# Striking scores in PSUM with TensorE, and moving their reading and two additions to other engines

## The chip, the cores and the metric

The kernel runs on one core of a Trainium2 chip. The metric is the device time of one execution in microseconds; several executions are timed and their median is compared. One more execution was profiled; all rows below come from it.

## The reference

The input is 8 sequences of 512 tokens with 128 features. After a layer norm, `xn` goes into two branches whose results meet in `x + s * silu(f)`.

- `s`: an attention block with three sources (blocks of 4 tokens, 64 selected tokens, windows of 32), gated, projected and normalised.
- `f`: a product-key expert layer. This is the part that the change touches:

```python
q = (x @ Wq.T).reshape(b, n, 2, HEADS, DIM_KEY).transpose(2, 0, 1, 3, 4)
sim = jnp.einsum('pbnhd,hkpd->pbnhk', q, keys)        # 2 x 8 heads x 32 scores for a token
sx, ix = jax.lax.top_k(sim[0], TOPK)                  # the 16 largest of 32
sy, iy = jax.lax.top_k(sim[1], TOPK)
all_scores = (sx[..., :, None] + sy[..., None, :]).reshape(b, n, HEADS, TOPK * TOPK)
scores, pk_indices = jax.lax.top_k(all_scores, TOPK)
wd = W_down[pk_indices]
wu = W_up[pk_indices]
h = jax.nn.gelu(jnp.einsum('bnd,bnhkd->bnhk', x, wd), approximate=False)
h = h * jax.nn.softmax(scores, axis=-1)
return jnp.einsum('bnhk,bnhkd->bnd', h, wu)
```

`pk_indices` is a place in the 16 x 16 table of rank pairs, and only 50 pairs can be among the 16 largest sums, so 50 experts are enough.

## The kernel before

A tile is 128 tokens; there are 32, four to a sequence (a batch row). Each of the five engines runs a program of its own, written out by hand, and they meet at counting semaphores. From tile 4 on all of them run `turn(n)`, whose four forms j = 0 to 3 belong to the four tiles of a row; a turn also works on tiles n-1 to n-4, so a tile passes through a pipeline of five turns. Attention steps of the row are spread over the same turns.

The steps of tile n, in order:

1. TensorE, `scores`: 16 vectors of 32 scores for a token into PSUM bank `sim_bank[n % 2]`, 128 x 512. It waits for `sim_used` of tile n-2.
2. VectorE, `first_8`: 16 MAX8 instructions, the 8 largest of each vector, into `top[:, v, 0:8]`. `mark_above`: 1 in the bf16 tile `above` where a score is at least the eighth.
3. VectorE, `strike_above`: `rest` = score - 1e38 x mark, in SBUF.
4. VectorE, `sum_above`, `spill_above`, `put_ties`: the marks are counted, and 8 extra columns of `rest` get the eighth value as often as ties ask for it. The counts and the products of the counting lie in columns of the score's own PSUM bank, which is free by then; `put_ties` gives it back (`sim_used`).
5. VectorE, `next_8`: 16 MAX8 over the 40 columns of `rest`, ranks 9 to 16.
6. TensorE transposes the ranks (`top_columns`), ScalarE copies them out, TensorE forms the 50 gaps of each head (`pair_gaps`), ScalarE copies them into `gap[n % 4]`; VectorE finds the 16th smallest (`gaps_of_pairs`, `gaps_of_thirds`, `last_gaps`).
7. GpSimd, `past_of`: gap minus that, f32, into `past`. ScalarE, `side_of`: its sign, bf16, into `side`. TensorE transposes that (`transpose_sides`), ScalarE copies it to `sideT` (`take_sides`), GpSimd squares it (`square_of`), TensorE counts with both (`count_places`), ScalarE (`out_by_of`) and GpSimd (`drop_of`) drop the pairs that are out.
8. ScalarE takes the exponentials with their sums (`exps`, eight for a tile), VectorE inverts the sums (`invert_sums`), GpSimd weighs (`weigh`), adds head halves (`add_halves`, 8 heads to 4) and quarters (`add_quarters`, 4 to 2); TensorE transposes the two that are left (`expert_weights`). For the last four tiles TensorE adds some or all of the heads in PSUM instead.

VectorE's turn n is `strike_above(n)`, half of `first_8(n + 1)`, `sum_above`, `invert_sums(n - 4)`, `spill_above`, in j = 0 the row maxima of the attention scores, the other half of `first_8`, `put_ties`, `mark_above(n + 1)`, half of `next_8`, the gaps of tile n-1 with the other half between them.

The last tile takes `last_past_of` on VectorE instead of `past_of`, and ScalarE squares its sides from PSUM.

Of the kernel before, what the change touches and what calls it, by code (L numbers as in the profile page):

```python
# [83 lines left out]
def program(nc, x, wq, bq, wk, bk, wv, bv, wo, bo, wg, bg, wc, bc, ws, bs,  # L84
# [16 lines left out]
    with ctx:  # L101
# [6 lines left out]
        def sem(name):  # L108
# [112 lines left out]
        rest = sb("rest", [P, VECS, KEYS + 8])  # L221
# [4 lines left out]
        past = sb("past", [P, HEADS, CANDS])  # L226
        side = sb("side", [P, HEADS, CANDS], BF16)
# [8 lines left out]
        wgt4 = sb("wgt4", [P, HEADS // 2, CANDS])  # L236
        wgt2 = [sb(f"wgt2_{i}", [P, 2, CANDS]) for i in range(2)]
# [37 lines left out]
        above_done, struck, summed_above, spill_done = (  # L275
            sem(n) for n in ("above_done", "struck", "summed_above", "spill_done"))
        topT_ready, topT_out, gap_ready, gap_out = (sem(n) for n in ("topT_ready", "topT_out", "gap_ready", "gap_out"))
        slot_gap_done, last8_done, past_done, side_done = (
            sem(n) for n in ("slot_gap_done", "last8_done", "past_done", "side_done"))
# [7 lines left out]
        wgt_done, wgt4_done, wgt2_done, c_ready, c_out = (  # L287
            sem(n) for n in ("wgt_done", "wgt4_done", "wgt2_done", "c_ready", "c_out"))
# [106 lines left out]
        def _(pool):  # L395
# [13 lines left out]
            nc.gpsimd.tensor_copy(ident16[:, :], ident[:, :])  # L409
            nc.gpsimd.tensor_scalar(off_mean[:, :], ident[:, :], -1.0 / D, None, ALU.add)  # L410
# [108 lines left out]
            def add_halves(n):  # L519

                pool.wait_ge(wgt_done, n + 1)
                w = wgt[n % 2]
                nc.gpsimd.tensor_tensor(wgt4[:, :, :], w[:, 0:HEADS // 2, :], w[:, HEADS // 2:HEADS, :],  # L523
                                        ALU.add).then_inc(wgt4_done, 1)

            def add_quarters(n):
                pool.wait_ge(wgt4_done, n + 1)
                if n >= 2:
                    pool.wait_ge(c_ready, n - 1)
                nc.gpsimd.tensor_tensor(wgt2[n % 2][:, :, :], wgt4[:, 0:2, :], wgt4[:, 2:4, :],  # L530
                                        ALU.add).then_inc(wgt2_done, 1)
# [77 lines left out]
            def turn(n):  # L609
                b, j = divmod(n, TB)  # L610
                if j == 0:
# [4 lines left out]
                    add_quarters(n - 4)  # L616
# [4 lines left out]
                elif j == 1:  # L621
# [4 lines left out]
                    add_quarters(n - 4)  # L626
                    square_of(n - 2)
                elif j == 2:
# [6 lines left out]
                    add_quarters(n - 4)  # L635
                    square_of(n - 2)
                    norm2(b - 1)
                elif n < TILES - 1:
# [7 lines left out]
                    add_quarters(n - 4)  # L646
                    if b >= 2:
                        add_input(b - 2)
                else:
# [3 lines left out]
                    add_quarters(n - 4)  # L653
# [53 lines left out]
        def _(act):  # L707
# [23 lines left out]
            def side_of(n):  # L731

                if n < TILES - 1:
                    act.wait_ge(past_done, n + 1)
                else:
                    act.wait_ge(last_past, 1)
                if n >= 1:
                    act.wait_ge(sideT_ready, n)
                nc.scalar.activation(side[:, :, :], past[:, :, :], ACT.Sign).then_inc(side_done, 1)  # L739

# [8 lines left out]
            def take_sides(n):  # L749

                act.wait_ge(sideT_ready, n + 1)
                if n == TILES - 1:
                    nc.scalar.activation(last_sideT[0:TWO, :], t_bank[0:TWO, :], ACT.Copy).then_inc(sideT_out, 1)
# [66 lines left out]
            side_of(0)  # L820
# [96 lines left out]
            def last_squares():  # L917
                nc.scalar.activation(last_squareT[0:TWO, :], t_bank[0:TWO, :], ACT.Square).then_inc(last_square, 1)
# [67 lines left out]
            def turn(n):  # L986
                b, j = divmod(n, TB)
                if j == 0:
# [3 lines left out]
                    side_of(n - 2)  # L992
# [9 lines left out]
                elif j == 1:  # L1002
# [3 lines left out]
                    side_of(n - 2)  # L1006
# [8 lines left out]
                elif j == 2:  # L1015
                    out_by_of(n - 3)
                    side_of(n - 2)
# [10 lines left out]
                elif n < TILES - 1:  # L1028
# [3 lines left out]
                    side_of(n - 2)  # L1032
# [6 lines left out]
                else:  # L1039
# [3 lines left out]
                    side_of(n - 2)  # L1043
# [11 lines left out]
            side_of(1)  # L1055
# [15 lines left out]
            side_of(TILES - 2)  # L1071
# [5 lines left out]
            side_of(TILES - 1)  # L1077
# [17 lines left out]
        def _(dve):  # L1095
# [76 lines left out]
            def mark_above(n):  # L1172

                dve.wait_ge(sim_top8, n + 1)
                if n >= 1:
                    dve.wait_ge(summed_above, n)
                nc.vector.tensor_tensor(above[:, :, :], sim_bank[n % 2][:, :].rearrange("p (v k) -> p v k", k=KEYS),  # L1177
                                        eighth(n, KEYS), ALU.is_ge).then_inc(above_done, 1)

            def strike_above(n):  # L1180

                dve.wait_ge(above_done, n + 1)
                if n >= 1:
                    dve.wait_ge(top_done, 2 * n)
                nc.vector.scalar_tensor_tensor(rest[:, :, 0:KEYS], above[:, :, :], STRUCK,  # L1185
                                               sim_bank[n % 2][:, :].rearrange("p (v k) -> p v k", k=KEYS),
                                               ALU.mult, ALU.add).then_inc(struck, 1)

            def sum_above(n):

                dve.wait_ge(struck, n + 1)
# [3 lines left out]
            def tie_slots(n):  # L1195
                return sim_bank[n % 2][:, TIES:TIES + 8 * VECS].rearrange("p (v k) -> p v k", v=VECS)
# [9 lines left out]
            def put_ties(n):  # L1206

                dve.wait_ge(spill_done, n + 1)
                nc.vector.scalar_tensor_tensor(rest[:, :, KEYS:KEYS + 8], tie_slots(n), SPILL, eighth(n, 8),
                                               ALU.mult, ALU.min).then_inc(sim_used, 1)  # L1210

            def next_8(n, h):
                dve.wait_ge(sim_used, n + 1)
                for v in range(h * HALF_V, (h + 1) * HALF_V):
                    last = nc.vector.max(top[n % 3][:, v, 8:16], rest[:, v, :])  # L1215
# [135 lines left out]
            def turn(n):  # L1351
                b, j = divmod(n, TB)
                strike_above(n)
                if n + 1 in tiles:
                    first_8(n + 1, [0])
                sum_above(n)
                invert_sums(n - 4)
                spill_above(n)
                if j == 0:
                    maxima(b - 1)  # L1360
                if n + 1 in tiles:
                    first_8(n + 1, [1])
                put_ties(n)
                if n + 1 in tiles:
# [25 lines left out]
            def last_past_of(m):  # L1390
                dve.wait_ge(last8_done, m + 1)
                dve.wait_ge(side_done, m)
                nc.vector.tensor_tensor(past[:, :, :], gap[m % 4][:, :, :],
# [116 lines left out]
        def _(pe):  # L1510
# [61 lines left out]

            def top_columns(n):
# [18 lines left out]
            def transpose_sides(n):  # L1592
                pe.wait_ge(side_done, n + 1)
# [5 lines left out]
                for k in range(HEADS // 2):  # L1599
                    last = mm(dst[0:TWO, bass.ts(k, P)], side[:, 2 * k:2 * k + 2, :].rearrange("p h c -> p (h c)"),  # L1600
# [17 lines left out]
            def expert_weights(n):  # L1618
# [9 lines left out]
                if n < TILES - TB:  # L1628
                    pe.wait_ge(wgt2_done, n + 1)
                    last = nc.tensor.transpose(o, wgt2[n % 2][:, :, :].rearrange("p h c -> p (h c)"), ident[:, :])  # L1630
                else:
                    if n == TILES - TB:
                        pe.wait_ge(wgt4_done, n + 1)
                        w, heads = wgt4, HEADS // 2
                    elif n < TILES - 1:
                        pe.wait_ge(wgt_done, n + 1)
                        w, heads = (wgt if n < TILES - LAST else last_wgts)[n % 2], HEADS
                    else:
# [352 lines left out]
```

## Time and profile before

| | |
|---|---|
| median of 3 runs | 278.73 us (277.35 to 278.85) |
| the profiled execution | 277.19 us, its span 275.4 us |
| VectorE (DVE) busy | 261.0 us, 95% |
| TensorE (PE) busy | 237.8 us, 86% |
| ScalarE (ACT) busy | 234.9 us, 85% |
| GpSimd (POOL) busy | 225.9 us, 82% |
| mean granted TensorE clock | 0.988 of full speed |

The span goes from the first to the last instruction; the execution's own time is 1.8 us longer. Busy time of an engine is the time in which an instruction of its own runs, waits left out. The first 58 us are set-up and the first four tiles; then come seven rows of four turns; the last 27 us finish what is left in the pipeline.

### The profile page before, as it was taken

To read this page: it belongs to the slowest core of one execution; us is meant where nothing else is said; L and a number is where in the kernel's file an instruction comes from. 1 tells how busy PE (TensorE), PEld (TensorE's weight loads), DVE (VectorE), ACT (ScalarE), POOL (GpSimd) and SP (SyncE) were. 2 spreads that over 40 slices of the span, in tenths; PEclk is the share of its full clock that TensorE was granted. 3 is DMA by queue.
4 is the path that set the end of the run, shared out by engine and by line. 5 is a ranking of instruction groups with operands and counts; after the bars stand their busy time and mean duration, and the time that the engine had idled before them with its cause. 6 is when DMAs were issued, how large, how long until landed. Compare 5 with 4: busy or idle time off the path is not lost.

```text
span 275.4 us, 7038 instructions
## 1 busy us (share of the span) xinstructions
PE 237.8 (86%) x1562; PEld 176.2 (64%) x1562; DVE 261.0 (95%) x1715; ACT 234.9 (85%) x1048; POOL 225.9 (82%) x344
## 2 busy tenths in 40 slices
PE   7799689897989988988898889988998899898891
PEld 7456343685668666765676577657765776587780
DVE  5899999999999999999999999999999999998985
ACT  2553866989899999999989999999999999998953
POOL 7889701467588979998999889988998899889972
PEclk9999999999899999999999999999999999999997
DMA  7930000000000000100000000100010001000102
GB/s 179 281 80 1 2 0 0 2 1 0 5 0 0 5 0 1 38 6 0 2 12 31 1 0 2 42 0 5 0 39 4 1 0 40 2 1 4 38 4 76
DMA packets 11228, 6.23 MB, mean 23 GB/s; under 512 B 1457, under 2 KB 10674, under 8 KB 11186
## 3 DMA queue, kind: packets, MB, share of 16 engines
q1 hardware_dynamic: 9858, 5.12, 7.0%
q10 hardware_dynamic: 1328, 0.66, 1.1%
q8 instruction: 13, 0.21, 0.3%
q14 instruction: 29, 0.24, 0.3%
HBM read 3.67 MB, written 2.10 MB: 21 GB/s over the span
## 4 chain that ended last, share of the span: by engine, by line
POOL 29%; PE 29%; ACT 22%; issue 14%; DVE 5%; POOLq 0%; ACTq 0%; DVEq 0%
POOL past L487 4%; PE scratch L1662 4%; PE sim L1570 4%; POOL squareT L502 4%; ACT prob L847 3%; POOL drop L509 3%; POOL wgt L515 3%; PE s_bank L1764 3%; PE s_bank L1758 2%; ACT gap L769 2%; ACT spare L866 2%; PE t_bank L1588 2%; PE s_bank L1553 2%; POOL wgt L523 2%; ACT side L739 2%
## 5 line engine op out<-in xcount | busy, mean ns | idle before, releaser
L1215 DVE MAX8 top<-rest 128x8 f32<-128x40 f32 x512 | 57.4, 191 | 0.1
L1165 DVE MAX8 top<-sim 128x8 f32<-128x32 f32 x496 | 54.0, 184 | 0.0
L847 ACT ACTIVATE prob<-drop 128x50 f32<-128x50 f32 x224 | 51.5, 254 | 0.0
L847 ACT ACTIVATION_READ_ACCUMULATOR prob<-drop 128x1 f32 x224 | 46.9, 211 | 0.0
L502 POOL TENSOR_TENSOR squareT<-sideT 100x512 bf16<-100x512 bf16 x31 | 32.6, 1050 | 4.8 <-ACT sideT L757 4.8
L487 POOL TENSOR_TENSOR past<-gap,last 128x400 f32<-128x400 f32 x31 | 26.8, 864 | 9.5 <-DVE last L1239 9.5
L1570 PE MATMUL sim<-sim_w,xT_all 128*128 128x512 f32 x64 | 33.9, 611 | 0.5 <-ACT xT_all L794 0.5
L509 POOL TENSOR_TENSOR drop<-gap,out_by 128x400 f32<-128x400 f32 x30 | 31.0, 1033 | 1.2 <-ACT out_by L746 1.2
L1588 PE MATMUL t_bank<-gaps_of,topT 128*128 128x200 f32 x128 | 30.1, 359 | 2.0 <-ACT topT L762 2.0
L515 POOL TENSOR_TENSOR wgt<-prob,rden 128x400 f32<-128x400 f32 x30 | 25.7, 856 | 5.9 <-DVE rden L1157 5.9
L1239 DVE MAX8 last<-slot_gap 128x8 f32<-128x22 f32 x256 | 24.4, 169 | 1.1
L1588 PEld LDWEIGHTS t_bank<-gaps_of,topT 128*128 128x128 f32 x128 | 20.8, 193 | 5.5 <-ACT topT L762 3.2
L1192 DVE TENSOR_REDUCE sim<-above 128x16 f32<-128x512 bf16 x32 | 21.9, 683 | 0.1
L1177 DVE TENSOR_TENSOR above<-sim,top 128x512 bf16<-128x512 f32 x32 | 21.8, 683 | 0.1
L1614 PE MATMUL f_bank<-count_s,sideT 101*128 101x100 bf16 x124 | 15.1, 208 | 7.8 <-POOL squareT L502 7.8
L1185 DVE SCALAR_TENSOR_TENSOR rest<-above,sim 128x512 f32<-128x512 bf16 x32 | 21.4, 669 | 0.1
L1614 PEld LDWEIGHTS f_bank<-count_s,sideT 101*128 101x128 bf16 x124 | 11.5, 98 | 15.1 <-issue 14.9
L757 ACT ACTIVATE sideT<-f_bank 100x512 bf16<-100x512 f32 x31 | 18.8, 607 | 0.7 <-PE f_bank L1600 0.5
L769 ACT ACTIVATE gap<-t_bank 128x400 f32<-128x400 f32 x32 | 16.1, 503 | 3.5 <-PE t_bank L1588 2.1
L739 ACT ACTIVATE side<-past 128x400 bf16<-128x400 f32 x32 | 17.1, 536 | 1.9 <-POOL past L487 1.8
L523 POOL TENSOR_TENSOR wgt<-wgt 128x200 f32<-128x200 f32 x29 | 17.7, 609 | 1.2
L1600 PE MATMUL f_bank<-ident,side 128*100 128x128 bf16 x124 | 13.1, 229 | 5.6 <-ACT side L739 5.3
(295 smaller groups left out, 755.7 us busy)
## 6 DMA issues: line engine op xcount, KB each, us to landing
out<-y_sb SPq DMA_DIRECT2D x7, 256.0 KB, 2.3
x_sb<-in_L_attn_hidden_states SPq DMA_DIRECT2D x2, 256.0 KB, 3.8
fwq_sb<-in_L_ffn_Wq ACTq DMA_DIRECT2D x2, 256.0 KB, 5.6
x_sb<-in_L_attn_hidden_states SPq DMA_DIRECT2D x1, 512.0 KB, 5.3
wc_sb<-in_L_attn_Wc SPq DMA_DIRECT2D x1, 256.0 KB
out<-last_y SPq DMA_DIRECT2D x2, 128.0 KB, 1.9
wo_in<-in_L_attn_Wo SPq DMA_DIRECT2D x1, 192.0 KB
keys_sb<-in_L_ffn_keys ACTq DMA_DIRECT2D x1, 128.0 KB, 3.3
```

What stands on the lines that cost most here:

```text
L487: nc.gpsimd.tensor_tensor(past[:, :, :], gap[n % 4][:, :, :], last8[n % 2][:, :, 7:8].to_broadcast([P, HEADS, CANDS]), ALU.subtract).then_ ...
L502: nc.gpsimd.tensor_tensor(squareT[0:TWO, :], sideT[0:TWO, :], sideT[0:TWO, :], ALU.mult).then_inc(square_done, 1)
L509: nc.gpsimd.tensor_tensor(drop[:, :, :], gap[n % 4][:, :, :], out_by[:, :, :], ALU.add).then_inc(drop_done, 1)
L515: nc.gpsimd.tensor_tensor(w[:, :, :], prob[n % 2][:, :, :], rden[n % 2][:, :].unsqueeze(2).to_broadcast([P, HEADS, CANDS]), ALU.mult).then ...
L523: nc.gpsimd.tensor_tensor(wgt4[:, :, :], w[:, 0:HEADS // 2, :], w[:, HEADS // 2:HEADS, :], ALU.add).then_inc(wgt4_done, 1)
L847: last = nc.scalar.activation(prob[d][:, h, :], drop[:, h, :], ACT.Exp, scale=-1.0, accum_out=den[d][:, h:h + 1])
L1165: last = nc.vector.max(top[n % 3][:, v, 0:8], sim_bank[n % 2][:, bass.ts(v, KEYS)])
L1215: last = nc.vector.max(top[n % 3][:, v, 8:16], rest[:, v, :])
L1239: last = nc.vector.max(last8[n % 2][:, h, :], slot_gap[:, h, :])
L1570: mm(sim_bank[n % 2][:, :], xT_all[:, bass.ts(n, P)], sim_w[:, :], start=True, stop=True).then_inc(sim_ready, 1)
L1588: last = mm(t_bank[:, bass.ts(k, HALF_H * CANDS)], topT[:, bass.ts(k, P)], gaps_of[:, :, :].rearrange("p h c -> p (h c)"), start=True, sto ...
L1614: mm(o, one[0:TWO + 1, bass.ts(k, P)], count_s[0:TWO + 1, :], start=True, stop=False)
```

## The change

- TensorE's new `strike(n)` adds -1e38 x mark to the scores where they lie in PSUM, with a constant `strike16` that GpSimd makes at the start. ScalarE's new `take_struck(n)` copies the struck scores to `rest[n % 2]`, now two buffers, and gives the bank back. Both stand first in their engine's turn. In tiles 0 to 3 VectorE still strikes.
- The counts (`counts`) and what `spill_above` makes (`tie`) now lie in SBUF. On VectorE `strike_above` leaves the turn, `spill_above` comes ahead of `invert_sums`, and `put_ties` ahead of the second half of `first_8`.
- `side_of` is gone: `past` is bf16, TensorE transposes it as it is, and ScalarE takes the sign when it copies the transposed differences out of PSUM.
- `add_quarters` is gone: TensorE adds the two pairs of heads in PSUM with two accumulating matmuls against the identity, where it transposed one pair.
- The last tile's differences are taken from the gaps in PSUM, and the square of its signs from `last_sideT`.

```diff
+        rest = [sb(f"rest{i}", [P, VECS, KEYS + 8]) for i in range(2)]
+        strike16 = sb("strike16", [P, P], BF16)
+        counts = sb("counts", [P, VECS])
+        tie = sb("tie", [P, VECS, 8])
-        side = sb("side", [P, HEADS, CANDS], BF16)
+        past = sb("past", [P, HEADS, CANDS], BF16)
+            nc.gpsimd.tensor_scalar(strike16[:, :], ident[:, :], STRUCK, None, ALU.mult)
...
             def past_of(n):
-                    pool.wait_ge(side_done, n)
+                    pool.wait_ge(sideT_ready, n)
...
-            def side_of(n):
-                nc.scalar.activation(side[:, :, :], past[:, :, :], ACT.Sign).then_inc(side_done, 1)
...
-                nc.scalar.activation(sideT[0:TWO, :], f_bank[0:TWO, :], ACT.Copy).then_inc(sideT_out, 1)
+                nc.scalar.activation(sideT[0:TWO, :], f_bank[0:TWO, :], ACT.Sign).then_inc(sideT_out, 1)
+
+            def take_struck(n):
+                act.wait_ge(struck, n - TB + 1)
+                act.wait_ge(top_done, 2 * n - 2)
+                nc.scalar.activation(rest[n % 2][:, :, 0:KEYS], sim_bank[n % 2][:, :].rearrange("p (v k) -> p v k", k=KEYS),
+                                     ACT.Copy).then_inc(sim_used, 1)
...
             def mark_above(n):
+                    if n <= TB:
+                        dve.wait_ge(sim_used, n)
+                    else:
+                        dve.wait_ge(struck, n - TB)
...
             def sum_above(n):
-                nc.vector.tensor_reduce(sim_bank[n % 2][:, 0:TIES], above[:, :, :], AX_X, ALU.add
-                                        ).then_inc(summed_above, 1)
+                nc.vector.tensor_reduce(counts[:, :], above[:, :, :], AX_X, ALU.add).then_inc(summed_above, 1)
...
-                nc.vector.scalar_tensor_tensor(tie_slots(n),
-                                               sim_bank[n % 2][:, 0:TIES].unsqueeze(2).to_broadcast([P, VECS, 8]), 2.0,
+                nc.vector.scalar_tensor_tensor(tie[:, :, :], counts[:, :].unsqueeze(2).to_broadcast([P, VECS, 8]), 2.0,
                                                rank_row[:, 7:15].unsqueeze(1).to_broadcast([P, VECS, 8]),
...
-                nc.vector.scalar_tensor_tensor(rest[:, :, KEYS:KEYS + 8], tie_slots(n), SPILL, eighth(n, 8),
-                                               ALU.mult, ALU.min).then_inc(sim_used, 1)
+                nc.vector.scalar_tensor_tensor(rest[n % 2][:, :, KEYS:KEYS + 8], tie[:, :, :], SPILL, eighth(n, 8),
+                                               ALU.mult, ALU.min).then_inc(ties_done, 1)
...
             def turn(n):
-                strike_above(n)
+                sum_above(n)
                 if n + 1 in tiles:
                     first_8(n + 1, [0])
-                sum_above(n)
+                spill_above(n)
                 invert_sums(n - 4)
-                spill_above(n)
                 if j == 0:
                     maxima(b - 1)
+                put_ties(n)
                 if n + 1 in tiles:
                     first_8(n + 1, [1])
-                put_ties(n)
...
+            def strike(n):
+                pe.wait_ge(above_done, n + 1)
+                mm(sim_bank[n % 2][:, :], strike16[:, :], above[:, :, :].rearrange("p v k -> p (v k)"),
+                   start=False, stop=True, skip_group_check=True).then_inc(struck, 1)
...
             def expert_weights(n):
-                    last = nc.tensor.transpose(o, wgt2[n % 2][:, :, :].rearrange("p h c -> p (h c)"), ident[:, :])
+                    pe.wait_ge(wgt4_done, n + 1)
+                    w, heads = wgt4[n % 2], HEADS // 2
+                for h in range(0, heads, 2):
+                    last = mm(o, w[:, h:h + 2, :].rearrange("p h c -> p (h c)"),
+                              ident[:, :], start=(h == 0), stop=(h == heads - 2))
```

## Rows read from the trace of the kernel before

**Rows 1.** Windows of one batch row: busy us (instructions), then clock, DMA share.
```profile
162.95:191.10 28.15, 24.91 (x171) 19.01 (x171) 27.53 (x196) 27.12 (x132) 26.28 (x36) 1.00 0.04 12
```
**Rows 2.** Timeline, VectorE: start us, us, line, operation; one row, first and last turn.
```profile
57.91 0.63 DVE L1185 SCALAR_TENSOR_TENSOR rest<-above,sim 128x512 f32<-128x512 bf16 x1
...
163.63 0.68 DVE L1185 SCALAR_TENSOR_TENSOR rest<-above,sim 128x512 f32<-128x512 bf16 x1
...
164.22 0.89 DVE L1165 MAX8 top<-sim 128x8 f32<-128x32 f32 x8
...
165.73 0.30 DVE L1201 SCALAR_TENSOR_TENSOR sim<-sim,rank_row 128x128 f32<-128x128 f32 x1
...
166.72 0.28 DVE L1209 SCALAR_TENSOR_TENSOR rest<-sim,top 128x128 f32<-128x128 f32 x1
...
166.91 0.69 DVE L1177 TENSOR_TENSOR above<-sim,top 128x512 bf16<-128x512 f32 x1
...
170.28 0.67 DVE L1185 SCALAR_TENSOR_TENSOR rest<-above,sim 128x512 f32<-128x512 bf16 x1
...
178.35 0.67 DVE L1185 SCALAR_TENSOR_TENSOR rest<-above,sim 128x512 f32<-128x512 bf16 x1
...
185.00 0.67 DVE L1185 SCALAR_TENSOR_TENSOR rest<-above,sim 128x512 f32<-128x512 bf16 x1
...
248.08 0.68 DVE L1185 SCALAR_TENSOR_TENSOR rest<-above,sim 128x512 f32<-128x512 bf16 x1
```
**Rows 3.** Timeline, ScalarE, third turn of the row.
```profile
187.33 0.55 ACT L739 ACTIVATE side<-past 128x400 bf16<-128x400 f32 x1
...
189.66 0.62 ACT L757 ACTIVATE sideT<-f_bank 100x512 bf16<-100x512 f32 x1
```
**Rows 4.** Timeline, TensorE, first turn of the row, and the tail.
```profile
171.13 0.30 PE L1696 MATMUL s_bank<-win_mask,ident 128*128 128x320 bf16 x1
...
171.26 1.01 PE L1700 MATMUL s_bank<-kw,qw 128*128 128x80 f32 x8
...
262.61 0.68 PE L1642 MATMUL sim<-ident,wgt 128*100 128x128 f32 x4
```
**Rows 5.** Timeline, GpSimd, the same row.
```profile
165.29 1.28 POOL L600 TENSOR_TENSOR y<-y,s_norm 128x512 f32<-128x512 f32 x1
...
171.49 0.88 POOL L487 TENSOR_TENSOR past<-gap,last 128x400 f32<-128x400 f32 x1
...
174.93 0.39 POOL L530 TENSOR_TENSOR wgt<-wgt 128x100 f32<-128x100 f32 x1
...
175.28 1.04 POOL L502 TENSOR_TENSOR squareT<-sideT 100x512 bf16<-100x512 bf16 x1
...
180.04 1.03 POOL L509 TENSOR_TENSOR drop<-gap,out_by 128x400 f32<-128x400 f32 x1
...
185.98 0.86 POOL L487 TENSOR_TENSOR past<-gap,last 128x400 f32<-128x400 f32 x1
```
**Rows 6.** Timeline, VectorE, tail.
```profile
257.28 1.62 DVE L1393 TENSOR_TENSOR past<-gap,last 128x400 f32<-128x400 f32 x1
...
269.05 1.22 DVE L1423 SCALAR_TENSOR_TENSOR nmr<-mv,rstd 128x2 f32<-128x2 f32 x1 [0.33 <-POOL rstd L698]
...
270.19 0.41 DVE L1468 SCALAR_TENSOR_TENSOR half_f<-f_bank,s_norm 128x256 f32<-128x256 f32 x1
...
270.63 0.42 DVE L1475 SCALAR_TENSOR_TENSOR last_y<-tanh_f,half_f 128x256 f32<-128x256 f32 x1
```
**Rows 7.** Timeline, GpSimd, tail.
```profile
257.20 1.27 POOL L606 TENSOR_TENSOR y_sb<-y,x_sb 128x512 f32<-128x512 f32 x1
...
258.43 1.37 POOL L502 TENSOR_TENSOR squareT<-sideT 100x512 bf16<-100x512 bf16 x1
...
268.98 1.26 POOL L606 TENSOR_TENSOR y_sb<-y,x_sb 128x512 f32<-128x512 f32 x1
```
**Rows 8.** Timeline, GpSimd, start.
```profile
2.71 0.55 POOL L410 TENSOR_SCALAR off_mean<-ident 128x128 f32<-128x128 f32 x1
```

More of the change, by code:

```diff
@@ L235, in program @@
         wgt = [sb(f"wgt{i}", [P, HEADS, CANDS]) for i in range(2)]
-        wgt4 = sb("wgt4", [P, HEADS // 2, CANDS])
-        wgt2 = [sb(f"wgt2_{i}", [P, 2, CANDS]) for i in range(2)]
+        wgt4 = [sb(f"wgt4_{i}", [P, HEADS // 2, CANDS]) for i in range(2)]
         last_drop = [sb(f"last_drop{i}", [P, HEADS, CANDS]) for i in range(2)]
@@ L286, in program @@
         half_out = sem("half_out")
-        wgt_done, wgt4_done, wgt2_done, c_ready, c_out = (
-            sem(n) for n in ("wgt_done", "wgt4_done", "wgt2_done", "c_ready", "c_out"))
+        wgt_done, wgt4_done, c_ready, c_out = (
+            sem(n) for n in ("wgt_done", "wgt4_done", "c_ready", "c_out"))
         last_past, last_square, last_kept, last_wgt, blocks_scaled = (
@@ L521, in add_halves @@
                 pool.wait_ge(wgt_done, n + 1)
[L522 to L527, printed above, removed]
                 if n >= 2:
                     pool.wait_ge(c_ready, n - 1)
-                nc.gpsimd.tensor_tensor(wgt2[n % 2][:, :, :], wgt4[:, 0:2, :], wgt4[:, 2:4, :],
-                                        ALU.add).then_inc(wgt2_done, 1)
+                w = wgt[n % 2]
+                nc.gpsimd.tensor_tensor(wgt4[n % 2][:, :, :], w[:, 0:HEADS // 2, :], w[:, HEADS // 2:HEADS, :],
+                                        ALU.add).then_inc(wgt4_done, 1)
             def gelu_times_weights(b):
@@ L752, in take_sides @@
                 if n == TILES - 1:
-                    nc.scalar.activation(last_sideT[0:TWO, :], t_bank[0:TWO, :], ACT.Copy).then_inc(sideT_out, 1)
+                    nc.scalar.activation(last_sideT[0:TWO, :], t_bank[0:TWO, :], ACT.Sign).then_inc(sideT_out, 1)
                     return
@@ L1627, in expert_weights @@
                 o = dst[0:TWO, bass.ts(n % TB, P)]
-                if n < TILES - TB:
-                    pe.wait_ge(wgt2_done, n + 1)
-                    last = nc.tensor.transpose(o, wgt2[n % 2][:, :, :].rearrange("p h c -> p (h c)"), ident[:, :])
-                else:
[L1632 to L1638, printed above, removed]
-                        pe.wait_ge(last_wgt, 1)
-                        w, heads = last_wgts[n % 2], HEADS
-                    for h in range(0, heads, 2):
-                        last = mm(o, w[:, h:h + 2, :].rearrange("p h c -> p (h c)"),
-                                  ident[:, :], start=(h == 0), stop=(h == heads - 2))
+                if n <= TILES - TB:
+                    pe.wait_ge(wgt4_done, n + 1)
+                    w, heads = wgt4[n % 2], HEADS // 2
+                elif n < TILES - 1:
+                    pe.wait_ge(wgt_done, n + 1)
+                    w, heads = (wgt if n < TILES - LAST else last_wgts)[n % 2], HEADS
+                else:
+                    pe.wait_ge(last_wgt, 1)
+                    w, heads = last_wgts[n % 2], HEADS
+                for h in range(0, heads, 2):
+                    last = mm(o, w[:, h:h + 2, :].rearrange("p h c -> p (h c)"),
+                              ident[:, :], start=(h == 0), stop=(h == heads - 2))
                 last.then_inc(c_ready, 1)
@@ L1772, in turn @@
                 b, j = divmod(n, TB)
+                strike(n)
                 if j == 0:
```

63 lines of the change are left out of this document (25 added, 38 removed).

## The prediction

> **What bounds the kernel now.** I read the busy times of one batch row (four turns, one per tile) first. Rows repeat every 28.15 us; in one of them VectorE is busy 27.53 us, ScalarE 27.12, GpSimd 26.28, TensorE 24.91 [rows 1]. So VectorE sets the pace with 0.62 us of waiting in a row, and ScalarE, at 1.03 us, stands right behind it. Tile 4's turn, the first of this kind, starts at 57.9 us and the last at 248.1 [rows 2], which is 6.76 such rows; what lies before and after is a head and a tail with limits of their own. Then I read VectorE's timeline through one row for the place of each instruction in its turn [rows 2], the GpSimd timeline of the same row [rows 5], and the tail, because there VectorE does for once what the change makes it do in every turn [rows 6, 7].
>
> **What VectorE loses and gains.** The strike goes: it stands 0.59 us ahead of the next instruction (163.63 to 164.22, [rows 2]), so 4 x 0.59 = 2.36 us in a row. The reduce, the spill and the ties stay, with their results in SBUF instead of PSUM. Ties now stand ahead of the second half of the first maxima, so the mark comes straight behind the maxima on which it waits. With an independent instruction between, the mark starts 0.09 us before the one ahead has ended (166.72 + 0.28 against 166.91, [rows 2]); an instruction that waits for the one ahead has no such overlap, and I charge 0.12 us a turn, 0.48 in a row (bounds: 0, and the 0.2 of a whole small slot). Unhindered, VectorE would then need 28.15 - 0.62 - 2.36 + 0.48 = 25.65 us for a row.
>
> **What those two small instructions now meet.** Before, the spill and the ties each read one operand in PSUM. After, both read two tensors in SBUF (counts and ranks; tie and top). Three rows of the tail show what that does beside a busy GpSimd. The last subtraction, 400 elements from two SBUF tensors, took 1.62 us; GpSimd's add had begun 0.08 us earlier and ended at 258.47, and VectorE ended 0.43 us after it at 258.90, which is just the time of 400 elements [rows 6, 7]. A scalar_tensor_tensor of two elements took 1.22 us beside a GpSimd add that ran from 268.98 to 270.24, and ended 0.03 us behind it; the spill, 128 elements with PSUM in it, takes 0.30 [rows 2]. And GpSimd's square right behind the first add took 1.37 us where others take 1.04 [rows 5, 7]. So a VectorE instruction with two SBUF inputs waits until GpSimd's running instruction has ended, and the reverse. The Trainium skill (SBUF — State Buffer, section Who interferes with whom) says the same of these two engines and adds that the one that starts first keeps the port for its whole instruction; the trace agrees with 1.62 and 1.22 us.
>
> What it costs depends on where the two fall. The spill comes 2.10 - 0.59 - 0.13 = 1.38 us after a turn's start (165.73 less 163.63, less the strike, less the reciprocal that now follows it), the ties 0.33 us behind the spill. I lay them on GpSimd's timeline as it stands [rows 2, 5]. Fourth turn (start 163.63): due at 165.01, past_of runs until 165.29, wait 0.3; the ties then meet the 1.28 us product, wait 1.1. First turn (170.28): past_of until 172.37, wait 0.7; the ties come behind the maxima and wait at most 0.1. Second (178.35): past_of until drop_of starts at 180.04, wait 0.3; the ties meet drop_of, 0.8. Third (185.00): past_of until 186.84, wait 0.45; then GpSimd itself waits for the reciprocal and the ties go through. Together 3.7 us in a row. But GpSimd is earlier once add_quarters is gone (0.35 us to the next instruction, [rows 5], and its own wait for the halves), until it meets its waits for VectorE. With it so much earlier the same exercise gives 1.1 (the product alone), 0.9, 0.6 and 0: 2.6 us. I take 3.0. The far bounds are nothing (GpSimd always waiting just then) and eight whole instructions, 8 x 0.73 (26.28 us in 36 instructions, [rows 1]), 5.8 us. GpSimd is held in turn for about 0.12 us eight times in a row, 1 us, less than the 1.4 that add_quarters gives back.
>
> Of VectorE's 0.62 us of waits I keep 0.2, since a later VectorE finds more ready. The row: 25.65 + 3.0 + 0.2 = 28.85 us, 0.70 more than now; 6.76 rows make +4.7 us.
>
> **The sources in SBUF.** Moving counts and ties out of PSUM I cost at nothing. Two scalar_tensor_tensor of 256 elements stand in the tail, one with an input in PSUM, 0.41 us, one with both in SBUF, 0.42 [rows 6]. Bounds: 0.02 us either way for each of three instructions. The Trainium skill (VectorE: DVE Perf Modes, section on the TRN2 errata) gives PSUM-sourced operations 62 cycles more of fixed cost than SBUF-sourced ones; an estimate by that page is 0.065 us for each of three, 0.78 us in a row, 5.2 us in all, and the sum would be 278.1. These rows do not bear it out.
>
> **ScalarE.** It loses the sign copy, 0.55 us for 400 elements from SBUF, and gains the copy of the struck scores, 512 elements from PSUM like sideT's, 0.62 [rows 3]. Four times 0.07 is 0.28, so 27.4 us busy in a row of 28.85: hidden. The two Sign for Copy swaps change nothing that a row shows. The new copy heads the turn, ahead of out_by, which in the third turn, its latest place, had ended when the sign copy started at 187.33 [rows 3], 2.3 us into VectorE's turn; VectorE needs it at the second maxima, about 3.3 us into a turn even without stalls. Slack of some 0.5 us, more with stalls. Behind it on ScalarE out_by and the top columns move by 0.5 us and are given it back where the sign copy stood.
>
> **TensorE.** The strike is one bf16 matmul of 512 columns; 320 columns in bf16 hold the engine 0.13 us (171.13 to 171.26, [rows 4]), so 0.21. It waits for a mark made in the turn before. The weights become two f32 matmuls, four records of 0.68 us together [rows 4], in the place of one transpose; I take the difference as 0.4 (bounds 0.2 and 0.68). Four of each: 24.91 + 0.84 + 1.6 = 27.35 us in the row. The transposes of the sides no longer wait for ScalarE's sign, which takes 0.5 us out of TensorE's waits. Hidden at 28.85, but without much cover. Scores for tile n+2 are released by ScalarE's copy instead of by the ties, that is, earlier in the turn: costed at nothing, and hidden by VectorE's second maxima if it should come late.
>
> **Head and tail.** GpSimd makes one more constant in its first chain; its neighbour took 0.55 us [rows 8], nothing there hides it: +0.5. In the tail the last subtraction reads PSUM (up to 1.1 us less) and the last sign copy (0.55 us, [rows 3]) is gone, but TensorE and ScalarE have work of other tiles between these steps, and the last square now waits for the sign: -0.6, bounds 0 and -1.6.
>
> Sum against the profiled execution: 277.19 + 4.7 + 0.5 - 0.6 = 281.8 (span 275.4 with 1.8 around it). The median of the three runs lies 1.54 above that execution; the same +4.6 on it gives 283.3 us.
>
> **Rivals.** (A) The forecast, with waits of 2.6 to 3.7 us in a row: rows of 28.45 to 29.55, 280.7 to 288.1. Chance 0.42.
> (B) Faster: GpSimd, with add_quarters gone, stands waiting when the spill and ties come, as it did in the third turn. It decides below 28.15 - 25.65 - 0.2 = 2.3 us of stalls in a row, 0.29 per instruction. ScalarE then sets the pace at 27.4 and, with 0.4 of waits, rows of 27.8: 6.76 x -0.35 - 0.1 = -2.5, so 276.2. For it: GpSimd idles 1.9 us in a row already. Against: the product of 1.28 us and drop_of lie across the places. Chance 0.20.
> (C) No phase helps: a spill that comes at random waits for half of an instruction, 0.37 us by the mean of 0.73 and 0.44 as the long ones are met more often, and the ties meet the next one nearly whole, 0.6. 4.1 us in a row: 29.95, +12.2 - 0.1, 290.8. Chance 0.17.
> (D) TensorE takes over: 27.35 us busy, and its present waits of 3.24 us in a row halve: about 29.0, 283 to 285, with VectorE waiting for TensorE or ScalarE instead of for GpSimd. Chance 0.11.
> (E) The fixed cost of PSUM sources is real and pays the stalls: 278.1, no change. Chance 0.10.
>
> **The numbers.** A change of 0.5%, 1.4 us, is about what a measurement can tell from none. Slower: A but for 0.04 of it, C and D, 0.66. Same: E and 0.04 of A, 0.14. Faster: B, 0.20. The range runs from 276.5, about B's middle, to 290, about C's, which leaves out half of each, 0.19.
>
> **What would show it.** Right: the spill and ties, 300 and 276 ns now, with means of 500 to 800 ns and ends a few hundredths behind a GpSimd instruction's; GpSimd spans longer by 0.1 here and there; TensorE's strikes near 0.3 us with no wait; sum and maxima unchanged. Wrong: spill and ties near 300 ns, or VectorE idle ahead of the second maxima on ScalarE's copy, or ahead of its row maxima on TensorE.

## The result and the profile after

The changed kernel takes 286.12 us (median of 4 runs, 284.79 to 287.37), the kernel before 278.04 beside it (4 runs, 277.33 to 278.85): a ratio of 1.0277, 95% interval 1.0235 to 1.0319. The forecast was 283.3, slower. The four executions come in two pairs: 284.79 and 284.97 us at a mean granted clock of 0.994 and 0.997, 287.26 and 287.37 us at 0.982; the profiled one, with a span of 284.8 us against 275.4, is of the second pair.

The page of the changed kernel, busy time of each engine and then the chain that ended last:

```profile
PE 248.6 (87%) x1659; PEld 190.9 (67%) x1674; DVE 255.7 (90%) x1687; ACT 236.1 (83%) x1044; POOL 218.3 (77%) x317
...
PEclk9999999999999999999999999999997999889997
...
PE 38%; ACT 28%; POOL 15%; issue 11%; DVE 6%; another core or an unknown queue 0%; POOLq 0%; DVEq 0%; ACTq 0%
```

The same chain line on the page of the kernel before:

```profile
POOL 29%; PE 29%; ACT 22%; issue 14%; DVE 5%; POOLq 0%; ACTq 0%; DVEq 0%
```

There, too, VectorE had 5% of the chain, though it was busy for 95% of the span.

No engine is as full as VectorE was before: VectorE fell from 261.0 us busy (95% of the span) to 255.7 (90%), and TensorE, ScalarE and GpSimd are at 87, 83 and 77%. Windows of one batch row, two undisturbed ones and one in which the granted clock fell (columns as in [rows 1]):

```profile
122.96:152.10 29.14, 26.19 (x187) 21.05 (x188) 27.20 (x194) 27.41 (x131) 25.17 (x32) 1.00 0.04 11
152.10:181.22 29.12, 26.18 (x187) 21.04 (x188) 27.19 (x193) 27.40 (x131) 25.15 (x32) 1.00 0.03 10
196.97:227.51 30.54, 27.64 (x190) 22.02 (x189) 26.64 (x195) 27.62 (x132) 25.14 (x32) 0.94 0.03 10
```

A row is 0.97 to 0.99 us longer than the 28.15 of [rows 1], and VectorE now stands idle for 1.94 us of it, where before it was 0.62. The span is 9.4 us longer. From the mark of tile 4 to that of tile 31, 6.75 rows, it is 7.95 us. About 2.4 of these go with two falls of the granted clock, near 216 and 247 us, the first of which makes its row 30.54 us long instead of 29.14; the other 5.6 are the longer rows. Before tile 4's mark the changed kernel loses 1.0 us, and behind tile 31's 0.5.

The two small VectorE instructions that got two SBUF inputs, all 32 of each (busy us, mean ns | idle before):

```profile
L1186 DVE SCALAR_TENSOR_TENSOR tie<-counts,rank_row 128x128 f32<-128x128 f32 x32 | 11.7, 366 | 0.1
L1195 DVE SCALAR_TENSOR_TENSOR rest<-tie,top 128x128 f32<-128x128 f32 x32 | 16.3, 509 | 0.1
```

Before, they took 299 and 277 ns on average. Two places in VectorE's timeline, and GpSimd's beside them:

```profile
189.18 0.67 DVE L1179 TENSOR_REDUCE counts<-above 128x16 f32<-128x512 bf16 x1
190.07 0.88 DVE L1146 MAX8 top<-sim 128x8 f32<-128x32 f32 x8 [0.23 <-PE sim L1556]
190.87 0.82 DVE L1186 SCALAR_TENSOR_TENSOR tie<-counts,rank_row 128x128 f32<-128x128 f32 x1
...
213.50 0.27 DVE L1186 SCALAR_TENSOR_TENSOR tie<-counts,rank_row 128x128 f32<-128x128 f32 x1
213.70 0.19 DVE L1138 RECIPROCAL rden<-den 128x8 f32<-128x8 f32 x1
213.81 0.29 DVE L1195 SCALAR_TENSOR_TENSOR rest<-tie,top 128x128 f32<-128x128 f32 x1
...
229.40 1.24 DVE L1195 SCALAR_TENSOR_TENSOR rest<-tie,top 128x128 f32<-128x128 f32 x1
```
```profile
190.68 0.87 POOL L488 TENSOR_TENSOR past<-gap,last 128x400 bf16<-128x400 f32 x1
...
213.81 1.19 POOL L510 TENSOR_TENSOR drop<-gap,out_by 128x400 f32<-128x400 f32 x1 [0.62 <-ACT out_by L727]
...
229.17 1.32 POOL L596 TENSOR_TENSOR y<-y,s_norm 128x512 f32<-128x512 f32 x1
```

The spill that meets `past_of` ends at 191.69, 0.14 us behind it (191.55). The ties that meet the 1.32 us product end at 230.64, 0.15 behind it (230.49). All 19 of the 64 that took more than 0.36 us, but for one in the first tiles, end 0.14 to 0.16 us behind a GpSimd instruction. Where GpSimd waited for ScalarE, at 213.2 to 213.8, both went through in 0.27 and 0.29, and GpSimd's `drop_of`, 1.03 us in the other turns, took 1.19 beside the ties.

The waits from 75 to 265 us, total us, times, longest:

```profile
POOL squareT L503 <- ACT sideT L738: 13.4, 15, 1.8
...
POOL drop L510 <- ACT out_by L727: 6.9, 12, 1.2
PE t_bank L1580 <- ACT topT L750: 6.3, 13, 0.7
DVE slot_gap L1211 <- ACT gap L757: 6.2, 7, 1.2
...
DVE nmax L1280 <- PE s_bank L1698: 5.3, 6, 1.4
...
DVE top L1146 <- PE sim L1556: 4.1, 5, 1.8
```

VectorE waits for TensorE's block scores and scores and for ScalarE's gaps, which it hardly did before (2.0 us for the block scores, 0.2 for the gaps). And the chain of the changed kernel from 206 to 228 us (start, us, what), read downwards, goes through the very instructions that were added. The granted clock was down to 0.50 in a part of this stretch (216 to 220 us), which lengthens the TensorE pieces there:

```profile
207.93 0.50 ACT gap L757
...
210.78 0.63 ACT prob L834 x6
...
212.86 0.48 ACT rest L744
213.34 0.39 ACT out_by L727
213.73 0.27 ACT topT L750
...
215.31 0.39 ACT gap L757
215.70 0.59 ACT pT_win L844
...
216.33 2.02 PE scratch L1653 x4
218.34 0.85 PE c_bank L1633 x4
219.20 1.31 PE sim L1556 x2
...
220.88 0.22 PE sim L1562
...
225.37 0.63 ACT sideT L738
226.07 1.04 POOL squareT L503
```

The copy of the struck scores (L744), the weights' matmuls (L1633, four records) and the strike (L1562) all lie on it. VectorE does not. The chain of the row before that, at a clock of 1.00, has the same steps: the copy at 154.61, the weights at 159.54 for 0.44 us, the strike at 161.21. From 119 to 150 us the chain of the kernel before has no piece of VectorE either.

### The profile page after: what moved, and what is told of

Read it like the earlier page. It is cut to its first block, busy times and chain, and to the rows that moved or that the text cites. A ratio compares the mean times of both kernels' runs of the same rounds, so it can differ in the third digit from the quotient of the medians.

```text
span 284.8 us, 7316 instructions
## 1 busy us (share of the span) xinstructions
PE 248.6 (87%) x1659; PEld 190.9 (67%) x1674; DVE 255.7 (90%) x1687; ACT 236.1 (83%) x1044; POOL 218.3 (77%) x317
## 4 chain that ended last, share of the span: by engine, by line
PE 38%; ACT 28%; POOL 15%; issue 11%; DVE 6%; another core or an unknown queue 0%; POOLq 0%; DVEq 0%; ACTq 0%
ACT prob L834 5%; PE scratch L1653 4%; PE sim L1556 4%; POOL squareT L503 4%; PE t_bank L1580 3%; ACT away L969 3%; PE s_bank L1755 3%; ACT gap L757 3%; ACT p_win L934 3%; PE c_bank L1633 2%; PE s_bank L1749 2%; PE s_bank L1691 2%; ACT spare L853 2%; PE s_bank L1539 2%; POOL wgt L516 2%
## 5 line engine op out<-in xcount | busy, mean ns | idle before, releaser
L488 POOL TENSOR_TENSOR past<-gap,last 128x400 bf16<-128x400 f32 x31 | 26.9, 868 | 15.8 <-PE f_bank L1595 14.5
L510 POOL TENSOR_TENSOR drop<-gap,out_by 128x400 f32<-128x400 f32 x30 | 31.9, 1064 | 8.7 <-ACT out_by L727 8.6
L1580 PE MATMUL t_bank<-gaps_of,topT 128*128 128x200 f32 x128 | 29.5, 353 | 8.7 <-ACT topT L750 8.6
L1556 PE MATMUL sim<-sim_w,xT_all 128*128 128x512 f32 x64 | 34.9, 628 | 0.5 <-ACT xT_all L782 0.5
L1179 DVE TENSOR_REDUCE counts<-above 128x16 f32<-128x512 bf16 x32 | 21.3, 667 | 0.0
L744 ACT ACTIVATE rest<-sim 128x512 f32<-128x512 f32 x28 | 17.0, 607 | 2.0 <-remote 0.8
L1633 PEld LDWEIGHTS c_bank<-ident,wgt 128*100 128x100 f32 x112 | 15.4, 176 | 4.7 <-issue 3.3
L1633 PE MATMUL c_bank<-ident,wgt 128*100 128x128 f32 x112 | 18.1, 287 | 0.3 <-POOL wgt L526 0.3
```

The costliest lines, as they stand in the source:

```text
L510: nc.gpsimd.tensor_tensor(drop[:, :, :], gap[n % 4][:, :, :], out_by[:, :, :], ALU.add).then_inc(drop_done, 1)
L1556: mm(sim_bank[n % 2][:, :], xT_all[:, bass.ts(n, P)], sim_w[:, :], start=True, stop=True).then_inc(sim_ready, 1)
L1580: last = mm(t_bank[:, bass.ts(k, HALF_H * CANDS)], topT[:, bass.ts(k, P)], gaps_of[:, :, :].rearrange("p h c -> p (h c)"), start=True, sto ...
L1633: last = mm(o, w[:, h:h + 2, :].rearrange("p h c -> p (h c)"), ident[:, :], start=(h == 0), stop=(h == heads - 2))
```

## The experiments

Two theories after the result. **Stalls**: the time is lost in VectorE's two instructions that now wait behind GpSimd (rival A of the prediction, which came nearest). **Loop**: TensorE's added work and the new copy lie in a loop of TensorE, ScalarE and GpSimd that has become longer than VectorE's row (rival D). First the change was taken apart; S is the strike with all that moves with it (counts and ties in SBUF, the copy, the new order of VectorE's turn), Q the quarters, G the signs. All kernels compute the whole reference.

**1. Signs alone.**

```diff
-                nc.scalar.activation(side[:, :, :], past[:, :, :], ACT.Sign).then_inc(side_done, 1)
...
-                nc.scalar.activation(sideT[0:TWO, :], f_bank[0:TWO, :], ACT.Copy).then_inc(sideT_out, 1)
+                nc.scalar.activation(sideT[0:TWO, :], f_bank[0:TWO, :], ACT.Sign).then_inc(sideT_out, 1)
```


> The kernel before with the signs alone: past in bf16, transposed as it is, the sign taken in ScalarE's copy. Theory 1 (the changed kernel is slow because VectorE's spill and ties wait for GpSimd): VectorE still sets the pace, rows of 28.15 us stay, only the tail is shorter: 277 to 278.5. Theory 2 (it is slow because TensorE and ScalarE have more to do and their results come late for each other and for VectorE): this part takes a step out of that loop, 275 to 278.

273.44 us, ratio 0.9838 (0.9761 to 0.9916), under the ranges of both theories. This part is a gain by itself.

**2. Quarters alone.**

```diff
-                    last = nc.tensor.transpose(o, wgt2[n % 2][:, :, :].rearrange("p h c -> p (h c)"), ident[:, :])
+                for h in range(0, heads, 2):
+                    last = mm(o, w[:, h:h + 2, :].rearrange("p h c -> p (h c)"),
+                              ident[:, :], start=(h == 0), stop=(h == heads - 2))
```


> The kernel before with the quarters alone: TensorE adds the two pairs of heads in PSUM, GpSimd's add_quarters is gone. Theory 1: no change, 277.5 to 279, as VectorE is the bound and nothing of it changes. Theory 2: TensorE has 0.4 us more in every turn, rows longer by 0.2 to 0.8 us, 279.5 to 284.

281.63 us, 1.0109 (1.0019 to 1.0199), as the loop has it. In a row GpSimd is busy for 24.92 us instead of 26.28 and TensorE for 25.95 instead of 24.91, and the row is 0.46 longer. (Here and below a row without a window is the time from one mark to the one four tiles later in VectorE's timeline, in rows at a clock of 1.00 from tile 11 on, which agree within 0.1: 28.15 us in the kernel before, 28.61 here, 27.65 with the signs.)

**3. Strike alone.**

```diff
-                strike_above(n)
+                sum_above(n)
...
+                mm(sim_bank[n % 2][:, :], strike16[:, :], above[:, :, :].rearrange("p v k -> p (v k)"),
+                   start=False, stop=True, skip_group_check=True).then_inc(struck, 1)
```


> The kernel before with the strike alone: TensorE strikes, ScalarE copies, counts and tie in SBUF, the new order on VectorE; side_of and add_quarters stay. Theory 1: about all of the loss, 284 to 288, with spill and ties at 0.35 to 0.5 us and rows near 29. Theory 2: ScalarE now has 0.5 us more in each turn and nothing given back; 29.5 us or more of it in a row, so also slow, 286 to 292, but with VectorE idle by 2 us in a row or more, waiting for gap, sim or the row maxima's scores.

294.32 us, 1.0522 (1.04 to 1.0643), above both ranges. Its profiled execution ran at a granted clock of 0.948 (span 294.8), so its rows of 30.73 us are not set beside the others; but ScalarE, which here has both the sign copy and the new one, is busy for 29.15 us in such a row, more than a whole row of the kernel before. The other three executions had a granted clock of 0.959 to 0.976, against 0.982 to 0.998 in those of the kernel before that it is compared with, so a part of the 5.2% goes with the clock.

**4. The kernel before, with nothing but counts and ties in SBUF.**

```diff
-                nc.vector.tensor_reduce(sim_bank[n % 2][:, 0:TIES], above[:, :, :], AX_X, ALU.add
+                nc.vector.tensor_reduce(counts[:, :], above[:, :, :], AX_X, ALU.add
...
-                return sim_bank[n % 2][:, TIES:TIES + 8 * VECS].rearrange("p (v k) -> p v k", v=VECS)
+                return tie[:, :, :]
```


> The kernel before with one thing changed: counts and tie lie in SBUF instead of columns of the score's PSUM bank. VectorE's order, its strike and everything on the other engines stay. It measures the stall by itself. Theory 1: spill and ties take 0.1 to 0.5 us more each, 6 to 12 us over 32 tiles, and as VectorE is full in a row they come out one for one: 284 to 290. Theory 2: the stall is small or is taken up by VectorE's waits, 278 to 281.

294.54 us, 1.059 (1.0513 to 1.0667), just above the range of the stalls: the same instructions in the same order, and 16 us more. Its VectorE groups:

```profile
L1215 DVE SCALAR_TENSOR_TENSOR rest<-tie,top 128x128 f32<-128x128 f32 x32 | 21.7, 677 | 0.2
...
L1207 DVE SCALAR_TENSOR_TENSOR tie<-counts,rank_row 128x128 f32<-128x128 f32 x32 | 17.7, 555 | 0.1
```

Against 277 and 299 ns that is 32 x (0.400 + 0.256) = 21 us of VectorE. 28 of the 64 took more than 0.36 us, and every one of them ends 0.14 to 0.16 us behind a GpSimd instruction. VectorE now has 58% of the chain. So the stall is real, and dear where VectorE sets the pace. This spoke for the stalls; the next pair does not.

**5 to 8. The parts in pairs, and the stall taken out.** Signs with quarters, and signs with strike; and from the changed kernel and from the latter, counts and ties put back in the scores' PSUM bank, behind ScalarE's copy:

```diff
-                nc.vector.tensor_reduce(counts[:, :], above[:, :, :], AX_X, ALU.add).then_inc(summed_above, 1)
+                dve.wait_ge(sim_used, n + 1)
+                nc.vector.tensor_reduce(sim_bank[n % 2][:, 0:TIES], above[:, :, :], AX_X, ALU.add
+                                        ).then_inc(summed_above, 1)
...
                     first_8(n + 1, [1])
+                sum_above(n)
+                spill_above(n)
+                put_ties(n)
```


> The changed kernel without its strike part: signs and quarters only, VectorE strikes, counts and ties in PSUM. The signs gave 4.5 us and the quarters cost 3. If TensorE's extra 0.4 us a turn costs because its results come late behind ScalarE's sign, it costs nothing here, where that sign is gone: 273 to 275. If the two just add: 276 to 277.5. Both theories of the whole change agree that this is well under it, so it gives the price of the strike part on this base.

> The changed kernel with one thing put back: counts and ties in columns of the score's own PSUM bank, once ScalarE has copied it; so that they come late enough, sum, spill and ties stand behind both halves of the first maxima. TensorE's strike, ScalarE's copy, signs and quarters stay as changed. Theory 1 (the waits for GpSimd are the loss): spill and ties at 0.28 to 0.30 us again, VectorE at 25 to 26 us in a row, rows of 27.6 to 28.2 set by ScalarE and TensorE, 273 to 278. Theory 2 (TensorE's and ScalarE's extra work and its lateness are the loss): rows of 29 or more remain, 283 to 287, with VectorE idle by 3 us in a row.

> The changed kernel with add_quarters put back on GpSimd and one transpose on TensorE. Theory 1: GpSimd is fuller by 1.4 us in a row, so spill and ties wait longer, 287 to 291. Theory 2: TensorE has 1.6 us less in a row, 281 to 285.

> The same as the one before, with counts and ties in PSUM as in the run before it. Theory 1: the fullest engine is ScalarE at 27.2 to 27.4 us in a row, rows of 27.5 to 28, 272 to 276, at or a little under the signs alone (273.4). Theory 2: 280 to 284.

| kernel | us | ratio (95%) | row | VectorE busy in it |
|---|---|---|---|---|
| 5 signs, quarters | 276.12 | 0.9953 (0.9935 to 0.997) | 28.19 | 27.57 |
| 7 signs, strike | 281.27 | 1.0133 (1.0098 to 1.0168) | 28.73 | 28.45 |
| 8 as 7, ties in PSUM | 280.29 | 1.009 (1.0055 to 1.0125) | 28.30 | 25.70 |
| 6 changed kernel, ties in PSUM | 285.07 | 1.0266 (1.0236 to 1.0295) | 29.02 | 25.80 |

Without quarters (7) VectorE works for 28.45 of 28.73 us and holds 51% of the chain, so there the stalls do bound the row. Yet taken away (8) they free 2.75 us of VectorE, and the row gives back 0.43, the time 1.0 us: another limit stands right behind. A part of that limit is the edit's own, for it also puts sum, spill and ties behind ScalarE's copy: the chain of kernel 8 runs from the copy at 217.44 us through them and the second maxima to 221.86. In the changed kernel (6) the same edit frees 1.4 us, the undisturbed row goes from 29.14 to 29.02, and the ratio, 1.0266, is that of the changed kernel, 1.0277, within both intervals (284.74 to 285.23 us, where the changed kernel took 284.79 and 284.97 at the same clock). Here the new order isn't on the chain: from 135 to 166 us it has pieces of TensorE and ScalarE alone. In kernel 7 GpSimd is busier than in the changed kernel and the stalls are longer (2.75 us in a row instead of 1.4), and yet the row is 28.73 us instead of 29.14. Windows of one row of signs alone, signs with strike, and the changed kernel with ties in PSUM, in this order:

```profile
130.91:158.55 27.64, 24.50 (x173) 18.89 (x172) 27.47 (x197) 25.54 (x128) 26.24 (x36) 1.00 0.04 11
```
```profile
134.08:162.81 28.73, 25.78 (x177) 19.45 (x176) 28.45 (x193) 27.28 (x132) 26.43 (x36) 1.00 0.04 11
```
```profile
135.24:164.26 29.02, 26.32 (x189) 21.06 (x188) 25.80 (x193) 27.40 (x132) 24.85 (x32) 1.00 0.04 10
```

In the last one VectorE is idle for 3.2 us, and its waits from 90 to 250 us have one great entry, for TensorE's block scores:

```profile
DVE nmax L1279 <- PE s_bank L1698: 14.5, 6, 2.5
```

**9 to 12. Is less of the change better?** With the signs, TensorE strikes only in the third turn (9), the fourth (10) or both (11), ties in PSUM there; 12 has both, and the quarters on TensorE in the first and third turns, in one of which TensorE had waited for GpSimd:

```diff
+        def pe_adds(n):
+            return n < TILES - TB and n % TB in (0, 2)
...
+        def pe_strikes(n):
+            return n >= TB and n % TB in (2, 3)
...
+                if pe_adds(n):
+                    return
```


> The kernel before with the signs, and TensorE's strike and ScalarE's copy in one turn of each row alone, the third (j = 2); VectorE strikes the other three tiles; counts and ties in PSUM, in the third turn behind ScalarE's copy. VectorE is at 27.5 us in a row of 27.64 with the signs alone and loses 0.35 to 0.59; ScalarE goes from 25.7 to 26.2, TensorE gets 0.21. If the loop through TensorE and ScalarE bears one strike: rows of 27.1 to 27.3, 270 to 272. If each strike costs what four cost (0.67 us a row for 28.31 against 27.64): 273.5 to 275.

> The same with the strike in the fourth turn (j = 3) instead of the third, where TensorE has its longest run between two waits for ScalarE. 270 to 272 if VectorE's time alone counts, 272 to 275 if the place in the loop does.

> The same with the strike in the third and the fourth turn. VectorE 26.5 to 26.8 us in a row, ScalarE 26.7. 268 to 271 if the loop bears it, 274 to 277 if the loop has taken over as with all four.

> Signs in ScalarE's copy, the strikes of the third and fourth turns added by TensorE with their ties left in PSUM, and the weights' quarters added by TensorE only for the first and third turns' tiles, GpSimd adding the others. If VectorE, GpSimd and the loop from TensorE over ScalarE to GpSimd stand side by side as limits near the signs kernel's row of 27.65 us, relieving VectorE by about 1 us and GpSimd by about 0.8 us a row gives rows of 27.1 to 27.4 us and 270 to 272.5 us, faster than the signs alone. If the loop through TensorE and ScalarE alone holds the row, what TensorE adds is paid and the time is 274 to 276 us, no better than the signs alone.

274.60, 274.13, 274.72 and 274.16 us; ratios 0.9888 (0.9851 to 0.9925), 0.9885 (0.9851 to 0.9919), 0.9894 (0.9871 to 0.9917) and 0.9885 (0.9843 to 0.9927). None is better than the signs alone, and each lies in the higher of its two ranges. In kernel 9's trace the rows vary from 27.33 to 27.98 us at a clock of 1.00, 27.68 on average. Row of 12:

```profile
131.21:158.80 27.59, 25.54 (x180) 20.09 (x180) 26.70 (x196) 26.22 (x129) 25.44 (x34) 1.00 0.04 12
```

VectorE has 0.77 us less to do than with the signs alone and GpSimd 0.80 less, and the row is the same within 0.05; TensorE has 1.04 more to do and ScalarE 0.68. The chain of 12 has ScalarE for 39% and TensorE for 36%, that of the signs alone GpSimd for 41% and VectorE for 27%, and in its settled rows (186 to 214 us) GpSimd alone. The same holds for kernel 10 (GpSimd 41%), whose VectorE has 0.5 us less to do and whose row is 27.63. So VectorE, busy for 27.47 of 27.64 us, did not hold that row: by the chain it was GpSimd's path in kernels 1 and 10, and TensorE's and ScalarE's in 11 and 12. That easing VectorE and GpSimd at this price would shorten the row is refuted; whether the second path was at 27.6 us already in kernel 1, or came to it by what was added, is not shown. Quarters in two turns cost nothing (27.62 against 27.66 and 27.7 in kernel 11), in all four 0.54 (28.19 against 27.65, on the signs alone). In one of the two turns TensorE's wait of 0.70 us for GpSimd's weights fell to 0.22 in kernel 12; that this is why it is free there was not tested turn by turn.

## Why the prediction was right in sign and size, and where not

Direction and range hold (283.3 forecast, 286.12 measured), and the row came out at 29.14 against 28.85. The rise was 8.1 us where 4.6 were forecast. That the row came so close is luck: two of its terms were wrong in opposite ways.

- **Strike off VectorE, mark's dependency: right as a sum.** Unhindered VectorE was to need 25.65 us; kernels 6 and 8, whose spill and ties take 299 and 291 ns, show 25.80 and 25.70, in another order of the turn.
- **Stalls behind GpSimd: mechanism right, term mis-sized.** 3.0 us in a row was charged. Over the run the two instructions grew by 67 and 232 ns, 0.30 a turn, 1.2 in a row; by the busy time of the row 27.20 - 25.80 = 1.4. Where VectorE is the pace-maker it is what was forecast: 28.45 - 25.70 = 2.75 in kernel 7 (2.6 to 3.7), and 2.6 in kernel 4. In the changed kernel GpSimd itself stands waiting for ScalarE (13.4 and 6.9 us, before 2.1 and 0.7) and is passed by. The ends lie 0.14 to 0.16 us behind GpSimd's, not a few hundredths, and the spill's mean is 366 ns, under the 500 that was to show it. The Trainium skill (SBUF — State Buffer, section Who interferes with whom) has the rule that the later of the two engines waits for the whole instruction of the earlier; these ends agree.
- **VectorE's other waits: the step that failed.** "Of VectorE's 0.62 us of waits I keep 0.2, since a later VectorE finds more ready", and of TensorE "Hidden at 28.85". Measured are 1.94 us of waits, for TensorE and ScalarE. Stalls and waits together are 3.34 us where 3.2 were charged: the sum held, its cause didn't. Taking all stalls away leaves a row of 29.02 (kernel 6), so what sets the time of the changed kernel is rival D, given 0.11, not A, given 0.42. D's sum, a row of about 29.0 and 283 to 285 us, is the nearest of the rivals', but it adds 27.35 us of work and 1.6 of waits, where 26.19 and 2.95 were measured: its mechanism is borne out, its sum is luck. The prediction's own sign of being wrong, VectorE idle ahead of its row maxima on TensorE, is there (5.3 us, before 2.0). The mistake begins in its first lines: VectorE "sets the pace" was read from the busy share, while the chain of the kernel before gave it 5%; it stood 0.62 us a row behind what held that kernel.
- **TensorE: busy time too high, its effect too low.** 27.35 us was forecast, 26.19 measured; 2.44 us was to come and 1.28 came (the trace of the changed kernel holds 13 of its 28 strikes; kernel 6, with all 28, shows 26.32), and the signs took 0.41 away (24.91 to 24.50), which the prediction had not counted. Still it isn't hidden, since it lies between a ScalarE result and the next ScalarE input. Step by step: quarters lengthen the row by 0.46 on the kernel before, 0.54 on the signs and 0.72 on kernel 8; the strike with ties in PSUM, so with no stall, by 0.65 on the signs and 0.83 on signs with quarters. How the strike's part divides between TensorE's matmul, ScalarE's copy and the new order was not tested. Busy share was read for cover; the chain would have been the view to read.
- **ScalarE: 0.28 us more in a row, measured 27.41 against 27.12: right. The claim that the copy is hidden: wrong.** The copy is on the chain at 212.86, between the probabilities and the top columns that TensorE waits for (6.3 us).
- **Signs: mis-sized.** Charged at -0.6 us in the tail and nothing in the rows. Alone it is worth 4.5 us by the ratio (2.3 to 6.6), and its rows are 0.5 shorter: VectorE's idle time in a row went from 0.62 us [rows 1] to 0.17 (27.47 of 27.64). That it came through TensorE's shorter waits, as the prediction had them but without a gain, was not tested by itself. In the tail of the changed kernel the last subtraction went from 1.62 us [rows 6] to 0.58. With the signs alone, the tail behind the last tile's mark is 0.5 us shorter, as charged; in the changed kernel it is 0.5 longer.
- **The clock: put at nothing.** About 2.4 us of the profiled execution go with two falls of the granted clock. The two executions at a mean granted clock of 0.994 and 0.997 took 284.9 us.
- **Sources in SBUF: right.** The reduce took 667 ns to SBUF and 683 to PSUM, and undisturbed the spill and ties took 0.27 and 0.29. Rival E is out.
- **Rival B** (faster) needed under 2.3 us of stalls in a row. That was met, with 1.2 to 1.4, and the kernel is slower all the same: its row of 27.8 left out what TensorE and ScalarE add between each other's steps.

The parts don't add: signs -1.6%, quarters +1.1, strike +5.2 make 4.7% where the whole change is 2.8%. The strike needs the signs, which take ScalarE's sign copy away (from +5.2% alone to 1.0133/0.9838, +3.0% on top of them). Open is which step of each path holds the 27.6 us of kernels 1 and 9 to 12, for no run eases GpSimd's path alone. How much of the 5.2% of the strike alone is ScalarE's load, how much the stalls and how much the clock was not separated either.

## What to carry to other kernels

When all engines are above 80% busy, the busiest one need not be the one that holds the time: VectorE was busy for 95% and had 5% of the chain. Taking work off it buys at most the gap to the next limit, and that limit can be a loop through several engines that no busy share shows. So look at the chain first, and before moving work onto an engine, look whether the new instruction falls where that engine waits anyhow (quarters in two turns cost nothing, in four 0.54 us a row) or between two steps of the loop. Undo a multi-part change part by part: here one part was a gain (the signs, -1.6%), which the other two hid. And where VectorE holds the time and GpSimd is busy beside it, keep one operand of small VectorE instructions in PSUM: it was worth 16 us in kernel 4, but only 0.12 us a row in the changed kernel, where VectorE was not on the chain.

## What the hardware showed that was not expected

- Two VectorE instructions of 0.3 us per turn, moved to SBUF operands and nothing else, cost 5.9% of the whole kernel, through waits behind GpSimd of 0.26 and 0.40 us on average.
- The wait works the other way too: `drop_of` took 1.19 us instead of 1.03 when it started with the ties. It never took more than 1.05 before, and never more than 1.06 in kernel 6, whose ties lie in PSUM.
- What a lower clock of TensorE cost here differed by whether TensorE was on the chain. In kernel 4, where VectorE holds the row, rows at a granted clock of 0.89 took 30.60 us, those at 1.00 took 30.57. In the changed kernel the row at 0.94 took 1.40 us more.
- In two rows of the changed kernel TensorE's granted clock went from 1.00 to 0.50 (the 1.2 GHz level) and came back, near 216 and 247 us. Windows of 1 us at the first:

```profile
215.00:216.00 1.00, 0.63 (x6) 0.39 (x5) 1.00 (x6) 1.00 (x3) 0.92 (x2) 1.00 0.00 0
216.00:217.00 1.00, 0.67 (x2) 0.31 (x2) 1.00 (x10) 1.00 (x5) 0.66 (x2) 0.78 0.00 0
217.00:218.00 1.00, 1.00 (x3) 0.79 (x3) 0.96 (x11) 1.00 (x4) 0.88 (x1) 0.50 0.00 0
...
220.00:221.00 1.00, 1.00 (x12) 0.63 (x10) 0.39 (x4) 0.89 (x4) 0.68 (x1) 1.00 0.00 0
```

Ahead of it TensorE had waited 0.72 us at 213.3 to 214.05 and 0.69 at 215.6 to 216.3, both for ScalarE. Two projections that take 0.72 us each in the row at 158 took 1.08 and 1.14. The row of the second fall has waits of 0.74 and 0.73 in the same places; the row at 158 has 0.74 and 0.69 and no fall, so the waits alone don't decide it. The windows compared above are at a clock of 1.00.
